# Maxima of the attention scores taken bank by bank, and exponents that wait for one bank

## What is computed

```python
scores = jnp.einsum('bhqd,bhkd->bhqk', q, k) / jnp.sqrt(jnp.asarray(HD, x.dtype))
scores = scores + causal_bias
attn = jax.nn.softmax(scores, axis=-1)
out = jnp.einsum('bhqk,bhkd->bhqd', attn, v)
out = out.transpose(0, 2, 1, 3).reshape(b, s, NH * HD)
return out @ wo
```

## Time and profile before

| | us |
|---|---|
| three runs before, median (lowest to highest) | 1962.02 (1958.76 to 1963.24) |
| the profiled execution, whole | 1962.85 |
| its span, first to last instruction | 1961.0 |
| its time outside the span | 1.85 |

### The profile page before, as it was taken

One profiled execution on the slowest core, in us unless ns is written; L12 is line 12 of the kernel. 1 busy time (PEld: TensorE's weight loads), 2 busy tenths in 40 slices (PEclk: granted clock), 3 DMA queues, 4 the chain that ended last, 5 costly groups with the idle time before them and its releaser, 6 DMA issues.

```text
span 1961.0 us, 36294 instructions
## 1 busy us (share of the span) xinstructions
PE 1894.9 (97%) x11088; PEld 1409.5 (72%) x11089; DVE 1181.4 (60%) x2901; ACT 1007.9 (51%) x3741; POOL 536.9 (27%) x704
## 2 busy tenths in 40 slices
PE   6999999999999999999999999999999999999994
PEld 5887887766668888766667888766667888766662
DVE  4676778543357888643357878643356888653345
ACT  4646776632336677632335766733335776642331
POOL 3752113340022322440022232440022333430023
PEclk9999999999999999999999999999999999999997
DMA  6422320231112330231121430231121340131123
GB/s 160 125 69 103 102 93 15 78 94 43 56 57 87 112 116 4 82 96 43 54 61 58 144 112 6 81 93 46 46 68 57 117 143 6 50 101 47 49 72 101
DMA packets 88760, 149.39 MB, mean 76 GB/s; under 512 B 13346, under 2 KB 64244, under 8 KB 88500
## 3 DMA queue, kind: packets, MB, share of 16 engines
q1 hardware_dynamic: 74664, 112.85, 18.5%
q0 software_dynamic: 13568, 34.27, 5.9%
q10 hardware_dynamic: 380, 0.38, 0.1%
HBM read 105.87 MB, written 41.59 MB: 75 GB/s over the span
## 4 chain that ended last, share of the span: by engine, by line
PE 76%; DVE 9%; ACT 7%; POOL 3%; issue 3%; DMA 1%; SPq 0%; POOLq 0%; DVEq 0%; ACTq 0%
PE ps L859 25%; PE ps L878 12%; PE ps L749 7%; ACT parena L1179 7%; PE ps L829 6%; PE ps L805 4%; PE ps L868 3%; PE ps L779 3%; PE ps L794 3%; PE ps L757 2%; PE ps L731 2%; POOL qk L547 2%; DVE rope L1499 2%; PE ps L853 2%; DVE rope L1503 2%
## 5 line engine op out<-in xcount | busy, mean ns | idle before, releaser
L859 PE MATMUL ps<-arena,xeT 128*128 x1120 | 527.9, 594 | 0.0
L1179 ACT ACTIVATE parena<-ps,nmax 112x112 f32<-112x112 f32 x1024 | 345.4, 389 | 105.3 <-DVE nmax L1520 105.3
L859 PEld LDWEIGHTS ps<-arena,xeT 128*128 128x128 f32 x1120 | 203.0, 192 | 141.6 <-issue 134.4
L547 POOL TENSOR_TENSOR qk<-qk,rope 128x448 f32<-128x448 f32 x128 | 146.3, 1143 | 555.1 <-DVE rope L1503 554.9
L1228 ACT ACTIVATE parena<-ps,er 128x512 f32<-128x512 f32 x140 | 96.2, 687 | 379.0 <-PE ps L859 375.5
L749 PE MATMUL ps<-xnT,wqk_s 128*128 128x224 f32 x1280 | 273.6, 357 | 0.0
L878 PE MATMUL ps<-arena,tarena 128*128 x1120 | 266.0, 380 | 1.9 <-issue 1.2
L526 POOL DMA_INDIRECT y_in<-sorted_y,pos x114 | 111.8, 980 | 543.9 <-DMA sorted_y<-tarena 402.3
L1179 ACT ACTIVATION_READ_ACCUMULATOR parena<-ps,nmax 112x1 f32 x1024 | 247.4, 242 | 0.0
L829 PE MATMUL ps<-wo_s,oT 128*112 128x256 f32 x1024 | 237.9, 385 | 1.4 <-issue 1.4
L749 PEld LDWEIGHTS ps<-xnT,wqk_s 128*128 128x128 f32 x1280 | 233.2, 191 | 2.9
(11 more groups left out here) (185 smaller groups left out, 2731.7 us busy)
## 6 DMA issues: line engine op xcount, KB each, us to landing
xe<-sorted_x SPq DMA_DIRECT2D x140, 130.0 KB, 2.1
sorted_y<-tarena SPq DMA_DIRECT2D x140, 128.0 KB
arena<-in_L_ffn_wg_dram SPq DMA_DIRECT2D x32, 512.0 KB, 3.7
arena<-in_L_ffn_wu_dram SPq DMA_DIRECT2D x32, 512.0 KB, 4.6
arena<-in_L_ffn_wd_dram SPq DMA_DIRECT2D x32, 512.0 KB, 5.5
arena<-in_ctx_dram SPq DMA_DIRECT2D x15, 375.0 KB
sorted_x<-tarena POOLq DMA_DIRECT2D x8, 568.8 KB, 4.5
qk<-in_L_ffn_wq_dram SPq DMA_DIRECT2D x4, 1024.0 KB
```

The source lines that it names most:

```text
L547: pool.tensor_tensor(q, q, rope[m % 2][:, :], ALU.add).then_inc(g_rope, 1)
L859: last = pe.matmul(ps[:, bank, :], xeT[u][:, k, :], w[:, bass.ds(e * 1024 + k * 512, 512)], start=(k == 0), stop=(k == KD - 1))
L1179: last = act.activation(prob[:, n, :], ps[0:S, bank, h * S:h * S + S], ACT.Exp, bias=nmax[:, b % 2, n:n + 1], scale=SCALE, accum_out=rsum[ ...
```

## The change

`maxima` takes each bank of four heads by an instruction of its own and scales it by an instruction of its own, which raises `d_max`; the semaphore so counts four per sequence in place of two, and `exponents` waits for it ahead of each bank's first head. `p_sc` is as before. The three totals of `Steps` grow by one for each call of `maxima`: 2 for the lead, 32 for a layer.

```diff
-DVE_LEAD = 8
-DVE_FIRST = 228
-DVE_LAYER = 239
+DVE_LEAD = 10
+DVE_FIRST = 260
+DVE_LAYER = 271
@@ exponents
-                act.wait_ge(d_max, l * 32 + 2 * b + p + 1)
                 for n in range(8 * p + n0, 8 * p + n1):
+                    if n % 4 == 0:
+                        act.wait_ge(d_max, l * 64 + 4 * b + n // 4 + 1)
@@ maxima
-                hs = slice(8 * p, 8 * p + 8)
-                step(dve.tensor_reduce(rmax[:, hs].rearrange("p (n h) -> p n h", n=2), heads(b, p), AX_X, ALU.max))
-                dve.tensor_scalar(nmax[:, b % 2, hs], rmax[:, hs], -SCALE, None, ALU.mult).then_inc(d_max, 1)
+                for j in range(2):
+                    hs = slice(8 * p + 4 * j, 8 * p + 4 * j + 4)
+                    bank = ps[0:S, score_bank(b, p) + j, 0:GN].rearrange("q (h k) -> q h k", k=S)
+                    step(dve.tensor_reduce(rmax[:, hs], bank, AX_X, ALU.max))
+                    dve.tensor_scalar(nmax[:, b % 2, hs], rmax[:, hs], -SCALE, None, ALU.mult).then_inc(d_max, 1)
```

## The result

The changed kernel takes 1975.62 us (median of 6 runs, 1973.97 to 1977.36) where the kernel before, timed beside it, takes 1963.21 (1958.76 to 1965.56): a ratio of 1.0064, 95% interval 1.0051 to 1.0077. It is slower by 12.4 us. The forecast was 1964.0 with a range up to 1969.0, so the forecast of no measurable change was wrong. The profiled execution took 1976.15 us with a span of 1974.3, 13.3 more than the span before.

A forecast was written before the change was run, and what follows sets the result against it. The prediction took TensorE to bound the kernel. Layer 0 at +0.38 and layers 1 to 3 at +0.53 each gave +2.0 us on the median of 1962.0, so 1964.0 us, range 1958.4 to 1969.

The forecast's parts named there:

- The price of a call: Call of `maxima` on VectorE: each 448-column maximum takes 0.620 us, the call goes from 1.20 to 1.47 us, 0.27 more.
- Iterations of odd b up to 9: Attention iterations on TensorE: there is room for the longer calls, so they stay at 14.60 us.
- b = 10 of layers 1 to 3: Division at b = 10: no room there, so the divided probabilities reach TensorE 0.15 us late in each of these layers.
- The positions: Places of the rows, L1678, after b = 11 and 12: end 0.60 us later in each layer.
- The gain of 0.05 us at b = 4, 6, 8 and 10: Second scores of even b on TensorE: come 0.05 us earlier at each of these b, 0.22 us a layer.
- The step that failed: From the positions to the first expert tile's turn: GpSimd's remaining scatters, landing, load and turn follow in fixed steps.
- the second rival: GpSimd's idle time or pauses between scatters: the delay is absorbed, giving 1961.6 us, or 1958.4 with earlier transfers; chance 0.17.
- The rival: Clock behind TensorE's waits of b = 14: three more layers lose 1.3 us each, giving 1967.9 us; chance 0.12.
- Exponents on the path: Exponents in the chain of waits: each of 60 iterations gives 0.47 us, 28 us in all, 1934 us; chance 0.07.
- Divisions by a costlier call: Odd b from 1 to 9, layers 1 to 3: calls over 0.34 us dearer make divided probabilities late, 1970.7 us; chance 0.06.
- The change does what it says: Rival claimed the opposite: an exponent waits for more than its bank, giving 1964.9 us; chance 0.03.

The follow-up runs named there:

- late division: Changed kernel with two VectorE instructions over 8 columns ahead of the division of p = 0 in b = 14: 1968.46 us, ratio 1.0026.
- late positions: Kernel before with three VectorE instructions over 8 columns ahead of the second set of places in b = 12: 1971.96 us, ratio 1.0046.
- the memsets: Kernel before with two GpSimd memsets over 64 columns ahead of the last scatter of the first kernel of positions in each layer: 1964.50 us, ratio 1.0007.
- the filling transposes: Changed kernel with four idle TensorE transposes ahead of the turn of the first expert tile at b = 14: 1975.57 us, ratio 1.0063.

## Why the prediction was wrong

**Right.** The price of a call: 0.620 us forecast, 0.619 measured, and 0.73 from one maximum to the next (809.54 to 810.27). Iterations of odd b up to 9 still take 14.60 us and gained nothing by the earlier exponents; b = 10 of layers 1 to 3 went from 15.65 to 15.85. The positions were forecast 0.60 later and came 0.66 later in the mean, from 0.17 to 1.42, since stalls of VectorE marked "issue" fell in other layers. The product of `rotate` for m = 3 ends 805.08 + 2.26 = 807.34, 0.48 behind GpSimd's sum (806.86), as it did before. The turn waits in all four layers, and it is the transfer that ends last there. Two smaller terms were off. The gain of 0.05 us at b = 4, 6, 8 and 10 did not come: the second scores of even b still start 1.24 to 1.26 us behind the first, as before, but for single stalls, so the -0.22 of each layer was nothing. And iteration 11 went from 14.66 to 15.18 us (15.53 in layer 3), since TensorE now waits 0.36 us for the first division there; no term had it, and it stays hidden, as TensorE stands before the transfer later on.

**The step that failed** is "The rest of GpSimd's scatters, their landing, the load at 812.40 and the turn at 814.68 follow in fixed steps". They took 1.52 us more in the mean of the layers, 6.1 in all, against a term of 0: scatters of b = 12 and 13 were held more often or longer, and the last took 1.81 us in place of 0.94. I had said in the second rival that scatters last 0.94 or 1.28 us "by what VectorE does beside them" and that the pattern moves, but used it only as a way to absorb a delay. It needed a price in both directions. Rows of before had it: GpSimd begins the last scatter 0.12 us ahead of a division of 1.09 us, and 0.22 us of shift between the two turned that round. That an earlier division can cost was in no term and no rival; the run with the change in b = 13 and 14 alone (+10.7) shows it, and the run that delayed the division (7.2 back) shows that this order, with what follows it, carries more than half of the whole.

**The clock.** The rival gave 1.3 us in each of three more layers. The trace has +1.46, +1.73 and +1.44 in layers 0 to 2, less 0.35 in layer 3, 4.3 in all. The effect was right and given 0.12; 4.3 us are a third of the whole. It followed from the first error: with waits of 1.3 us in all and 0.6 at most, in the run with the late division, layers 0 to 2 kept 1.00; with 1.2 to 1.3 us none did in the changed kernel's profiled execution. But the length of this wait doesn't decide alone. With waits of 1.2 to 1.3 us three of eight layers kept 1.00 (layer 1 with the change in all but b = 10 to 12, layers 0 and 2 with it in b = 13 and 14), while with 0.6 to 0.7 us layers 0 and 2 fell with the late positions, and layer 2 fell with the memsets without any wait for xe. The sums over four layers, each from one profiled execution, against the kernel before:

| | positions | to the issue | to the turn | to the scores of b = 15 | clock at 0.50 behind the turn |
|---|---|---|---|---|---|
| changed | +2.6 | +6.1 | -0.3 | +4.3 | layers 0 to 3 |
| all but b = 10 to 12 | +0.3 | +5.7 | -0.2 | +1.8 | 0, 2, 3 |
| b = 10 to 12 alone | +2.6 | +7.4 | -0.2 | -0.1 | 3 |
| b = 13 and 14 alone | +0.6 | +5.7 | -0.2 | +1.3 | 1, 3 |
| late positions | +2.0 | +5.1 | -0.4 | +2.7 | 0, 2, 3 |
| changed, late division | +2.0 | +3.4 | -0.3 | 0.0 | 3 |

The scatters' part is there each time, the clock's part comes and goes. How much of the 12.4 us the clock would cost by itself isn't settled, as the filling transposes didn't hold it up reliably.

**The other rivals.** Exponents on the path: no. The delay absorbed: no layer. Divisions by a costlier call: the call wasn't costlier, yet TensorE's waits for divisions went from 5.8 to 9.9 us; they didn't set the end, since the transfer came later still. The change does what it says.

**What stays open.** Late positions alone cost 8.9 us, the change in b = 13 and 14 alone 10.7, both together in the whole change 12.4, so they don't add up; by the traces it depends on which scatter is held in which layer, and no run takes the layers apart. The 5.2 us left with the late division are 2.0 of later positions (4 x 0.49), 3.4 of scatters held in b = 12 and 13 (4 x 0.86), and small terms of both signs; they were not taken apart by a run.

## What to carry to other kernels

When an edit shifts one engine by a few tenths of a microsecond beside a chain on another that shares something with it, list for each instruction of that chain what the neighbour has under way at its start and how near the edge is, and price the shift in both directions. Then ask what waits behind the chain, since the delay of one transfer here brought a slower clock with it. A span of several instructions whose durations vary in the trace of before is no fixed step. Freeing work earlier on an engine that isn't the bound is not free: it moves what that engine does beside others.

## What the runs showed of the hardware

**A GpSimd scatter waits at its start for a VectorE instruction with two inputs in SBUF.** The mean of the scatters by line, in the kernel before and, as the second fence, in the changed one:

```profile
L577 POOL DMA_INDIRECT sorted_x<-x_sb,pos_x x128 | 126.1, 985 | 108.1 <-DVE pos_x L1678 72.7 <-issue 35.4
```

```profile
L577 POOL DMA_INDIRECT sorted_x<-x_sb,pos_x x128 | 132.7, 1036 | 110.2 <-DVE pos_x L1681 74.8 <-issue 35.4
```

I went through the 128 scatters of each profiled execution and asked whether a VectorE `TENSOR_TENSOR` (product, sum or division) with both inputs in SBUF was under way when they began.

```
kernel                 begun under one   mean us   the others, median us
before                       20           1.19          0.94
changed                      32           1.31          0.94
changed, late division       28           1.24          0.94

changed kernel: left of VectorE's instruction at the start -> length of the transfer
0.299 -> 1.117     0.504 -> 1.317     0.631 -> 1.451     0.991 -> 1.807
```

Where over 0.13 us are left, the length is what is left plus 0.80 to 0.83 us, some 0.13 less than a free transfer takes; for the first scatter of a layer it is 0.92 to 0.96 more. Scatters that began with over 0.25 us left of a VectorE instruction that reads PSUM (maxima, L1501, products of the expert stage) were not held: 69 in the first two kernels, 0.95 us in the mean and 1.05 at most. The split maxima themselves so hold up no scatter. A division that begins 0.01 or 0.02 us after the transfer doesn't lengthen it, and one that begins 0.02 to 0.04 us ahead of it doesn't either (0.93 to 0.96 us, in the runs of the change in some iterations); one that begins 0.06 or 0.07 us ahead does (1.84 to 1.86 us).

The Trainium skill (SBUF — State Buffer, section Who interferes with whom) infers that `tensor_tensor` leaves descriptor generation alone because it takes only the read interface. These traces disagree for indirect transfers. They agree with another sentence of that section, that a VectorE instruction with two SBUF inputs contends with a GpSimd instruction that reads SBUF, if the transfer reads its indices there at its start; that reading was not tried by itself.

**The same program can order its engines otherwise on another chip.** One kernel had a ratio of 1.0040 on one chip and 0.9953 on another, with intervals far apart. On the second, waits marked remote of up to 8.5 us stand in that run's trace; that they are the reason wasn't tested.
